# One-hot tiles of a graph kernel: layout in interleaved pairs, low ones for eight cells at once, and the first batch counted ahead of the first group

## The reference

```python
h = relu(layernorm(x))
msg = where(edge_type == 0, h[src] @ W_data.T + b_data, h[src] @ W_control.T + b_control)
x = x + relu(segment_sum(msg, dst) + h @ W_self.T + b_self)
h = relu(layernorm(x))
norm = deg_inv_sqrt[src] * deg_inv_sqrt[dst]
out, y = h, h
for _ in range(2):
    y = segment_sum(y[src] * norm[:, None], dst)
    out = out + y
return x + out / 3
```

## Time and profile before

| | us |
|---|---|
| median of 3 runs | 3734.86 (3733.47 to 3736.71) |
| the profiled execution | 3728.22 |
| its span in the profile | 3726.5 |
| from its first gathered row to the last quads of pass 0, about | 167 to 1994 |

### The profile page before, as it was taken

One profiled execution on the slowest core, in us unless ns is written; L12 is line 12 of the kernel. 1 busy time (PEld: TensorE's weight loads), 2 busy tenths in 40 slices (PEclk: granted clock), 3 DMA queues, 4 the chain that ended last, 5 costly groups with the idle time before them and its releaser, 6 DMA issues.

```text
span 3726.5 us, 64465 instructions
## 1 busy us (share of the span) xinstructions
PE 3268.1 (88%) x23900; PEld 2911.8 (78%) x23900; DVE 1800.9 (48%) x4518; ACT 2671.9 (72%) x2895; POOL 2482.8 (67%) x2635
## 2 busy tenths in 40 slices
PE   5568889898989887777777999999998999999998
PEld 2357768677777765555556999999997999999998
DVE  4655563554454469889995233333333222222223
ACT  3426666676767655545556888899996899999997
POOL 3477666677677676777775666666664666666666
PEclk9869989999999886677777999999998999999999
DMA  8452322333333355555556778888889878877876
GB/s 246 142 160 79 104 87 83 110 99 93 99 108 87 98 187 192 180 192 179 194 179 209 227 230 245 247 251 251 251 242 322 245 229 235 236 230 237 235 232 200
DMA packets 444210, 694.31 MB, mean 186 GB/s; under 512 B 62391, under 2 KB 373570, under 8 KB 435700
## 3 DMA queue, kind: packets, MB, share of 16 engines
q1 hardware_dynamic: 343827, 447.82, 37.6%
q0 software_dynamic: 99200, 241.92, 23.0%
q10 hardware_dynamic: 864, 0.39, 0.0%
HBM read 514.92 MB, written 174.97 MB: 185 GB/s over the span
## 4 chain that ended last, share of the span: by engine, by line
PE 66%; DVE 17%; ACT 9%; issue 4%; DMA 2%; POOL 2%; DVEq 1%; SPq 0%; ACTq 0%; POOLq 0%
PE wide L1486 39%; PE turned_bank L1412 10%; PE sums_bank L1360 7%; PE wide L1398 6%; ACT typed_ring L1277 4%; DVE stage L1863 3%; PE sums_bank L1362 3%; DVE flat L1862 3%; DVE flat L1867 3%; ACT stage L1266 1%; ACT scaled L1196 1%; ACT strip_ring L1284 1%; DMA stage<-strips 1%; DMA h_rows<-flat 1%; DVE xin L1737 1%
## 5 line engine op out<-in xcount | busy, mean ns | idle before, releaser
L1117 POOL DMA_INDIRECT flat<-typed_table,index x1333 | 1296.2, 972 | 511.1 <-issue 406.9
L1284 ACT CAST strip_ring<-stage 128x1792 fp32r<-128x1792 uint8 x896 | 1495.8, 1688 | 144.4 <-PE wide L1486 124.3
L1486 PE MATMUL wide<-table_parts,strip_ring 128*128 128x256 f32 x12544 | 1542.6, 285 | 38.9 <-ACT strip_ring L1284 31.5
L1486 PEld LDWEIGHTS wide<-table_parts,strip_ring 128*128 128x128 f32 x12544 | 1528.0, 193 | 42.8 <-issue 25.9
L1117 POOL DMA_INDIRECT rows<-hop_table,index x1162 | 1111.2, 956 | 608.6 <-issue 314.8
L1266 ACT CAST stage<-wide 128x392 uint16<-128x392 f32 x1344 | 563.6, 496 | 530.5 <-PE wide L1398 528.2
L1398 PE MATMUL wide<-stage,flat 128*128 128x196 bf16 x2688 | 560.4, 353 | 205.1 <-DVE flat L1867 193.8
L1398 PEld LDWEIGHTS wide<-stage,flat 128*128 128x128 bf16 x2688 | 258.0, 122 | 474.7 <-DVE flat L1867 337.9
L1412 PE MATMUL turned_bank<-typed_ring,table_parts 128*128 128x256 f32 x3920 | 543.4, 299 | 70.6 <-ACT typed_ring L1277 63.3
L1828 DVE SCALAR_TENSOR_TENSOR sums<-sums_bank,in_upper,sums 128x128 f32 (+1 forms) x459 | 160.9, 351 | 892.5 <-PE sums_bank L1362 675.2
L1412 PEld LDWEIGHTS turned_bank<-typed_ring,table_parts 128*128 128x128 f32 x3920 | 514.7, 204 | 93.6 <-issue 57.0
(11 more groups left out here) (179 smaller groups left out, 1098.1 us busy)
## 6 DMA issues: line engine op xcount, KB each, us to landing
stage<-strips SPq DMA_DIRECT2D x896, 224.0 KB, 3.7
strips<-stage SPq DMA_DIRECT2D x64, 1568.0 KB
table_parts<-hop_table SPq DMA_DIRECT2D x28, 896.0 KB, 9.5
flat<-typed_table,index POOLq DMA_INDIRECT x1333
rows<-hop_table,index POOLq DMA_INDIRECT x1162
resid<-xin SPq DMA_DIRECT2D x50, 256.0 KB, 4.3
xin<-resid SPq DMA_DIRECT2D x50, 256.0 KB, 5.1
typed_table<-flat SPq DMA_DIRECT2D x49, 256.0 KB, 2.2
```

Of the source, the lines that this page charges most:

```text
L1117: pool.indirect_dma_start(out=gathered(k, o % RING, c), out_offset=None, in_=tables[k], in_offset=bass.IndirectOffsetOnAxis(ap=index[:, ch ...
L1284: act.copy(strip_ring[:, number % STRIP_RING], counts_ring[place]).then_inc(strip_cast, 1)
L1486: last = pe.matmul(wide[:, nth % 4, 0:PARTS * P], strip_ring[:, number % STRIP_RING, b - first, :], table_parts[:, b, :, :].rearrange("p n ...
```

## The change

Three things are changed. First, the layout of the one-hots: four cells stand as two pairs, `p (q n w) -> p q n w` with q = 2 and w = 2, so that a cell's matrix is every second 16-bit value of its half; the table in PSUM has every number twice. The same layout goes to the one-hots of the counts. Second, the low ones of plain tiles are made for eight cells by one compare and one weighting, at the even quad of two; the odd quad only compares its keys. Third, the small steps of slot 0 come ahead of the sum of group 0 on TensorE, the first batch's cells are fetched ahead of gather 3 and turned in slot 1, and work begins in slot 2; the costs by which work is spread are 1.6, 2.1 and 2.3 in place of 1.75, 2.3 and 2.4.

```diff
-WORK_START = 5
+WORK_START = 2
-QUAD_COST, TYPED_QUAD_COST, TYPED_STEP_COST = 1.75, 2.3, 2.4
+QUAD_COST, TYPED_QUAD_COST, TYPED_STEP_COST = 1.6, 2.1, 2.3
...
+    def low_place(quad, kind):
+        if quad < TYPED_TILES * QUADS:
+            return quad % 2, 2 * kind
+        return quad // 2 % 2, 2 * (quad % 2)
...
-        quad_hot = [region(QUAD * hot_columns // 2, BF16).rearrange("p (n w) -> p n w", w=QUAD) for _ in range(2)]
+        quad_hot = [region(QUAD * hot_columns // 2, BF16).rearrange("p (q n w) -> p q n w", q=2, w=2) for _ in range(2)]
...
-        quad_low = [[in_spare(QUAD * P // 2, BF16).rearrange("p (n w) -> p n w", w=QUAD) for _ in range(TYPES)] for _ in range(2)]
+        eight_low = [in_spare(2 * QUAD * P // 2, BF16).rearrange("p (q n w) -> p q n w", q=QUAD, w=2) for _ in range(2)]
...
             if s == 0:
-                fetch_slot.append(place_slot[0] + WORK_START - 1)
-                cells_turn_slot.append(fetch_slot[0])
+                fetch_slot.append(EARLY)
+                cells_turn_slot.append(WORK_START - 1)
...
+                        low, first = low_place(quad, kind)
                         for half in range(2):
-                            w = (2 * pair + half) % QUAD
                             made = pe.matmul(wide[:, nth % CELL_BANKS, half * hot_columns:(half + 1) * hot_columns],
-                                             quad_low[place][kind][:, :, w], quad_hot[place][:, :, w], start=True, stop=True)
+                                             eight_low[low][:, first + pair % 2, :, half], quad_hot[place][:, pair % 2, :, half],
+                                             start=True, stop=True)
...
+                        if k == 0 and i == 0:
+                            for kind, number in small_of_slot(i):
+                                small_step(kind, number)
                         if i < slots_of(k):
                             sum_group(first_of[k] + i)
...
-                            for kind, number in small_of_slot(i):
+                            for kind, number in small_of_slot(i) if i else ():
...
                     if quad >= 2:
                         dve.wait_ge(strip_made, keeps_through(quad - 2))
                     first = quad * QUAD % (CELL_BATCHES * P)
...
+                    hot_of = dict(out=quad_hot[place], in0=table(2, hot_columns), in1=by_cell(cell_key, 2, hot_columns), op=ALU.is_equal)
+                    low = low_place(quad, 0)[0]
                     if tile < TYPED_TILES:
-                        dve.tensor_tensor(typed_low, low, by_cell(cell_typed, P), ALU.mult)
-                    dve.tensor_tensor(low, low, by_cell(cell_weight, P), ALU.mult).then_inc(strip_hot_ready, 1)
+                        plain, typed_low = eight_low[low][:, 0:2], eight_low[low][:, 2:4]
+                        dve.tensor_tensor(plain, table(2, P), by_cell(cell_low, 2, P), ALU.is_equal).then_inc(low_raw, 1)
+                        dve.tensor_tensor(**hot_of)
+                        dve.wait_ge(low_raw, lows_through(quad))
+                        dve.tensor_tensor(typed_low, plain, by_cell(cell_typed, 2, P), ALU.mult)
+                        dve.tensor_tensor(plain, plain, by_cell(cell_weight, 2, P), ALU.mult).then_inc(strip_hot_ready, 1)
+                    elif quad % 2 == 0:
+                        dve.wait_ge(strip_made, keeps_through(quad - (2 if quad == TYPED_TILES * QUADS else 3)))
+                        dve.tensor_tensor(eight_low[low], table(QUAD, P), by_cell(cell_low, QUAD, P), ALU.is_equal).then_inc(low_raw, 1)
+                        dve.tensor_tensor(**hot_of)
+                        dve.wait_ge(low_raw, lows_through(quad))
+                        dve.tensor_tensor(eight_low[low], eight_low[low], by_cell(cell_weight, QUAD, P), ALU.mult).then_inc(strip_hot_ready, 1)
+                    else:
+                        dve.tensor_tensor(**hot_of).then_inc(strip_hot_ready, 1)
```

More of the change, by code:

```diff
@@ L420, in gnn_kernel @@
         typed_sums = xin[:, XIN - 1, TYPES * P:2 * TYPES * P]
-        count_hot = [scaled[:, 1, n * 2 * P:(n + 1) * 2 * P].bitcast(BF16).rearrange("p (n w) -> p n w", w=QUAD) for n in range(2)]
+        count_hot = [scaled[:, 1, n * 2 * P:(n + 1) * 2 * P].bitcast(BF16).rearrange("p (q n w) -> p q n w", q=2, w=2) for n in range(2)]
         count_marks = scaled[:, 0, 0:count_groups * CHUNKS].bitcast(I32)
@@ L475, in gnn_kernel @@
         counts = bank("counts", 1)[:, 0, :].bitcast(I32)
-        pair_words = real_blocks * QUAD
-        count_quads = counts[:, 0:pair_words].bitcast(I16).rearrange("p (n w) -> p n w", w=QUAD)
+        pair_words = hot_columns
+        count_pairs = counts[:, 0:pair_words].bitcast(I16).rearrange("p (n w) -> p n w", w=2)
         count_up = counts[:, pair_words:pair_words + P // 2].bitcast(I16)
@@ L1433, in count_group @@
                             chunk = c * CHUNKS + half * QUAD + w
-                            last = pe.matmul(count_columns, count_hot[half][:, :, w],
+                            last = pe.matmul(count_columns, count_hot[half][:, w // 2, :, w % 2],
                                              marks[:, chunk:count_groups * CHUNKS + 1:count_groups * CHUNKS - chunk],
@@ L1523, in _ @@
             twice = float((1 << 16) + 1)
-            dve.tensor_scalar(counts[:, 0:pair_words].rearrange("p (n w) -> p n w", w=QUAD // 2),
-                              iota[:, 0:hot_columns].unsqueeze(2).to_broadcast([P, hot_columns, QUAD // 2]), twice, None, ALU.mult
-                              ).then_inc(count_made, 1)
+            dve.tensor_scalar(counts[:, 0:pair_words], iota[:, 0:hot_columns], twice, None, ALU.mult).then_inc(count_made, 1)
             dve.tensor_scalar(counts[:, pair_words:pair_words + P // 2], iota[:, 0:P // 2], 2.0 * twice, float(1 << 16), ALU.mult, ALU.add
@@ L1847, in cut, with table, lows_through @@
                     dve.tensor_copy(sums[:, free, 0:CARRIED, :], sums[:, kept, NODE_BLOCKS:KEPT_TILES, :]).then_inc(cut_made, 1)
+                def table(pairs, columns):
+                    return count_pairs[:, 0:columns, :].unsqueeze(1).to_broadcast([P, pairs, columns, 2])
+                def lows_through(quad):
+                    typed = TYPED_TILES * QUADS
+                    return quad + 1 if quad < typed else typed + (quad - typed) // 2 + 1
                 def make_quad(quad):
@@ L1856, in make_quad @@
                     first = quad * QUAD % (CELL_BATCHES * P)
-                    def by_cell(values, columns):
-                        return values[:, first:first + QUAD].unsqueeze(1).to_broadcast([P, columns, QUAD])
-                    low, typed_low = quad_low[place]
-                    dve.tensor_tensor(low, count_quads[:, 0:P, :], by_cell(cell_low, P), ALU.is_equal).then_inc(low_raw, 1)
-                    last = dve.tensor_tensor(quad_hot[place], count_quads, by_cell(cell_key, hot_columns), ALU.is_equal)
@@ L1864, in make_quad, with by_cell @@
-                    dve.wait_ge(low_raw, quad + 1)
-                    if tile < TYPED_TILES:
-                        dve.tensor_tensor(typed_low, low, by_cell(cell_typed, P), ALU.mult)
-                    dve.tensor_tensor(low, low, by_cell(cell_weight, P), ALU.mult).then_inc(strip_hot_ready, 1)
+                    def by_cell(values, pairs, columns):
+                        return (values[:, first:first + 2 * pairs].rearrange("p (q w) -> p q w", w=2).unsqueeze(2)
+                                .to_broadcast([P, pairs, columns, 2]))
@@ L1872, in make_count_hot @@
                     first = c * CHUNKS + half * QUAD
-                    dve.tensor_tensor(count_hot[half], count_quads[:, 0:P, :],
-                                      local[:, first:first + QUAD].unsqueeze(1).to_broadcast([P, P, QUAD]), ALU.is_equal
+                    dve.tensor_tensor(count_hot[half], table(2, P), local[:, first:first + QUAD].rearrange("p (q w) -> p q w", w=2)
+                                      .unsqueeze(2).to_broadcast([P, 2, P, 2]), ALU.is_equal
                                       ).then_inc(count_hot_ready, 1)
@@ L1971, in _ @@
                 dve.wait_ge(ones_made, 2)
-                dve.tensor_scalar(cell_line, count_quads[:, 0:P, 0], float(P), None, ALU.mult).then_inc(cells_split, 1)
+                dve.tensor_scalar(cell_line, count_pairs[:, 0:P, 0], float(P), None, ALU.mult).then_inc(cells_split, 1)
                 dve.tensor_single_scalar(count_marks, index[:, 0:typed_chunks], 1, ALU.bitwise_and).then_inc(marks_made, 1)
```

## The result

Four runs of the changed kernel give a median of 3703.97 us (3697.34 to 3704.01), four of the kernel before beside it 3735.78 us: a ratio of 0.9911, 95% interval 0.9894 to 0.9928, some 32 us. The profiled execution took 3704.01 us, with a span of 3701.4 us. The forecast, 3710 us for a median and 3703 for an execution as fast as the one profiled before, lay close. It was close as a sum and wrong in two of its three terms, which fell on opposite sides; so a good part of the closeness is luck.

What follows compares the result with a forecast made beforehand. The prediction took the first pass to be bound by the chain TensorE, ScalarE, VectorE, not the gathers. Plain stage -5, typed stage -14 and start -6 made -25 us: a 3710 us median, range 3685 to 3727, or 3683 to 3757 with rival 1.

Steps and rivals of the forecast that it cites:

- Cells faster at full clock: TensorE's cell matmuls: a shorter reading step takes each from about 0.17 to 0.094 us at full clock.
- rival 1: TensorE's cells get no faster, as bank or type sets their 0.17 us; plain slots 10.16 us, whole 3756 us; chance 0.25.
- No gain at half clock: TensorE's cell matmuls at half clock stay as slow as before the change, about 0.17 us each.
- VectorE's costs in pairs: VectorE's compares keep their pace with runs of two: 0.60 us for 1024 elements, 0.47 for a key compare.
- rival 3: VectorE's runs of two take one element a cycle; a pair of quads costs 4.0 us, whole about 4040; chance 0.03.
- Plain stage: Slots making plain tiles: 9.3 to 9.6 us in place of 9.62, -5 us in all, ends -16 and +28.
- the replay: One plain slot stepped through VectorE and TensorE after the change: 9.29 us, 9.6 with late cells at half clock, 10.16 without faster cells.
- Full clock follows the sum and half clock comes after: TensorE in plain slots: cells right behind the group sum run at full clock, later ones at half; basis for 9.3 to 9.6 us.
- Rival 2: TensorE, idler, stays at half clock in the plain stage, +20 us, swallowing other gains; whole about 3733 us; chance 0.17.
- Typed stage, faster cells: Slots making typed tiles: faster cells shorten the ends of ScalarE-paced runs, -14 us, lower end 0, at most 27.
- Start: Start of the pass: first cells 15.5 us earlier, less 9 us of work now behind them, -6 us, ends -12 and 0.
- Gathers: POOL's gathers are no bound; moving group 3's gather delays those behind by 10 us, which TensorE's lag covers.

Runs made afterwards that it cites:

- layout_only: Kernel before with only the pair layout; low rows of four cells per quad, old schedule, costs and order: ratio 0.9944 to before.
- hot_pairs: Kernel before with only the key rows, the operand TensorE streams, in two interleaved pairs: ratio 0.9939 to before.
- no_eight: Changed kernel with low rows for four cells per quad in the plain stage too; pair layout, schedule and costs kept: ratio 0.9866 to before.
- layout_eight: Changed kernel with the schedule, costs and order of the kernel before; pair layout and eight-cell low rows kept: ratio 0.9996 to before.
- schedule_only: Kernel before with only the new schedule: first batch counted ahead of the first group, work from slot 2, new costs; ratio 0.9934 to before.
- low_pairs: Kernel before with only the low rows, the operand loaded as weights, in two interleaved pairs: ratio 0.9998 to before.
- costs_only_old: Changed kernel with the old costs 1.75, 2.3 and 2.4; start in slot 2 and first-slot order as changed: ratio 0.9933 to before.
- sum_first: Changed kernel with TensorE's sum of the first group again ahead of the first batch's counts; work still from slot 2: ratio 0.9915 to before.
- late_wait: Changed kernel with VectorE's wait in even plain quads moved from ahead of the low compare to behind it: ratio 0.9894 to before.
- four_late: Changed kernel with four-cell low rows in the plain stage, four buffers for them, and VectorE's wait behind the low compare: ratio 0.9858 to before.
- start_1: Changed kernel with four-cell low rows in the plain stage and work from slot 1 in place of 2: ratio 0.9880 to before.
- start_4: Changed kernel with four-cell low rows in the plain stage and work from slot 4 in place of 2: ratio 0.9882 to before.

## Why the prediction was right, and where it was not

- **Cells faster at full clock: right, in size too.** 0.094 us was taken from the hop's row; the median within plain quads is 0.089 in layout_only, 0.091 in hot_pairs and 0.100 in the changed kernel. The reason given, the reading step, is now shown by two runs and narrowed to the streamed operand. The Trainium skill ("SBUF — State Buffer", the cachelines note under The DMA port swizzle) lets bf16 stride by eight elements for free. It is the rule behind rival 1, and hot_pairs disagrees with it: from a step of four elements to one of two, four cells fell from 0.87 to 0.54 us. Rival 1 is thereby out.
- **"No gain at half clock": nearly.** Four cells take 0.84 us in the row above, against 0.88 before; the median distance within plain quads at 0.50 went from 0.176 to 0.162.
- **VectorE's costs in pairs: right.** Pitches of 0.60 and 0.47 us, as worked out; rival 3 is out. Its price came from the hot rows, whose results are of a wider type (fp32r), so that row was no pure case of short runs. The Trainium skill ("Vector Engine (DVE) Microarchitecture Reference", section 5.1) asks for a step of 1 and more than one element, and these pitches agree.
- **Plain stage: the sign was wrong.** Forecast -5 with ends -16 and +28, measured +9.4. In the slot shown above the replay had the right waits in the right places, but it let the cells behind the sum run at full clock, "0.91 less four times 0.08 = 0.59". That holds in other slots (0.55 in the one at 1676.87); here the clock was 0.52 and the release took 0.90 us. Its second key compare then came 5.16 us after the boundary (1832.08 to 1837.24), where the replay has 4.74 with faster cells and 5.06 without. The step that failed is "Full clock follows the sum and half clock comes after", read from one slot and given to all. Of the 50 plain slots whose cells begin right behind the sum, the first 0.6 us of cells lie at full clock (over 0.9) in 29 before and in 23 after, and at half clock (under 0.6) in 16 and 21 (in no_eight 31 and 10 of 49). So "9.3 to 9.6 is my reading" failed too: the 49 plain slots that hold no batch's finish (those under 11.5 us between two hot rows) average 9.65 us after; 49 such slots make 9.50 before and 9.17 in no_eight. Rival 2's mechanism, TensorE at half clock in this stage, was at work in part: 0.69 in the window, 389 us at half clock against 375.
- **The prediction compared the two edits as one.** It sets the eight-cell rows' 24 us of less VectorE work and the layout's faster cells against each other in a single replay. The runs take them apart: the layout was worth -16.0 there, the rows +26.9. Its own sentence on the 0.47 us between two even quads pointed at the rows as the risk; the next step, to ask what the layout would bring without them, was not taken.
- **Typed stage, faster cells: -14 forecast, -11.4 in layout_only, -15.6 in layout_eight, -14.3 in hot_pairs.** The size is right. TensorE's cells there took 250 us before and 197 after, counting each matmul from the end of the one before it; its idleness grew from 136.0 to 162.7, so half of what the cells saved came back as idleness. In layout_only, with the old schedule, it is more: the cells save 55 us, idleness takes 35 back, and the typed steps 11 (531.2 to 542.1). That ScalarE's copies set the pace was argued, and no run isolates it. ScalarE's waits for cells fell from 79 to 65 in layout_only and to 51 after:

```profile
ACT stage L1271 <- PE wide L1403: 222.6, 51, 66.5
```

- **Start: mis-sized, -6 forecast (ends -12 and 0), -24.8 in schedule_only.** What the step reckoned with came true: first cells 16.8 us earlier (15.5 forecast), and three more sums behind them, 8.8 us by the same count. The failing sentence is "the three slots gained and the new costs only spread the same typed work ... No time for that". From first cells to slot 105 schedule_only also lost 11.3 us of its typed steps' time (531.2 to 519.9) and 7.9 us of TensorE's idleness (136.0 to 128.1): -16.8 + 8.8 - 11.3 - 7.9 and 2.4 for cells and counts is -24.8. Together with the plain stage's miss, 14.4 us the other way, this is why the sum came out close.
- **What stays open** is why those steps got faster. The traces point to the clock: from first cells to slot 105 TensorE was at half clock for 167 to 222 us in the five kernels that begin the work in slot 5 (before, layout_only, layout_eight, hot_pairs, low_pairs), and for 140 to 157 us in the nine that begin it in slot 4 or earlier. The costs and the first slot's order are not the reason, as costs_only_old has 156 us and sum_first 155. The sizes are rough, as layout_only and layout_eight, with the same instructions there, have 222 and 197 us. Which step's new place brings the higher clock, no run isolates.
- **Gathers: right for this change.** Moving the gather of group 3 behind the first sum cost nothing that shows: the group sums of the kernel after wait 4.1 us for gathered rows in all, at its end, against 12.4 before. The cover is used up where the plain stage gets shorter: in it the sums wait 36.6 us in late_wait, 17.8 in four_late, 11.4 in start_1 and 3.0 in no_eight.

## What to carry to other kernels

Cost a layout and a restructuring that come in one change separately, each against the kernel without the other: here one was worth 16 us of a stage and the other took 27 away. When a double-buffered producer's work is bunched, saved instructions bring nothing if the producer waits longer for its consumer: here 13 us were saved and 29 more were waited. A wait belongs behind whatever doesn't need that buffer; moving one was worth 19.5 us of the stage. A replay of slots needs the granted clock of each step from many slots, since one slot's clock was not that of the others, and it changed together with the waits that were replayed. And when one engine's wait is removed, ask whose pace comes next: late_wait ran into the gathers.

## What the runs showed of the hardware that was not expected

The pace of a bf16 matmul of 196 columns hangs on the step of the streamed operand and hardly on that of the weights: at a clock of 1.00, a median of 0.176 us with both at four elements, 0.175 with the weights at two, 0.091 with the streamed operand at two and 0.089 with both. At 0.50 it is 0.176 and 0.175, and 0.162 with the streamed operand at two, alone or with both.

The same typed work, with the same instructions, got 140 to 157 us at half clock in start_1, start_4 and no_eight and 197 to 222 in layout_eight and layout_only, which differ there in the place of the steps alone; TensorE's typed steps took 542 us in layout_only and 525 in start_4.
